# A post-norm layer on one core: the FFN, the projections and V taken out of a stage of their own and put between the two heads' scores of each attention step

## The reference, cut to what matters

```python
# x: 8 batches of 1024 rows, 256 columns; H = 16 heads of D = 16
q, k, v = split(x @ w_qkv.T + b_qkv)
q, k = rope(elu(q) + 1), rope(elu(k) + 1)
attn_out = softmax(q @ k.T / sqrt(D)) @ v
x = layernorm(x + attn_out + depthwise_conv3(v) + b_lepe)
h = concatenate([x, -x])                 # k0, k1, k2 are sign matrices
h = relu(s0 * h @ sign(k0)) * 2          # 512 -> 1024
h = relu(s1 * h @ sign(k1)) * 2          # 1024 -> 1024
x = layernorm(x + s2 * h @ sign(k2))     # 1024 -> 256
```

## Time and profile before

| | before |
|---|---|
| median of 3 runs | 2331.88 us (2328.82 to 2332.24) |
| profiled execution, time | 2330.97 us |
| profiled execution, span | 2329.4 us |
| PE busy | 2144.3 us, 92% |
| DVE busy | 1530.3 us, 66% |
| ACT busy | 1429.2 us, 61% |
| POOL busy | 945.1 us, 41% |
| mean granted TensorE clock | 0.960 |

### The profile page before, as it was taken

The page is one execution under the profiler, slowest core; times in us unless marked ns, Lnnn a source line. Parts: engine busy times, 40 slices in busy tenths (PEclk is TensorE's granted clock), DMA queues, the critical chain, the costliest instruction groups (busy, mean ns, idle before and its releaser), DMA issues.

```text
span 2329.4 us, 41754 instructions
## 1 busy us (share of the span) xinstructions
PE 2144.3 (92%) x16960; PEld 835.0 (36%) x16960; DVE 1530.3 (66%) x1694; ACT 1429.2 (61%) x2605; POOL 945.1 (41%) x657
## 2 busy tenths in 40 slices
PE   4699899999899999999999999999999999998977
PEld 2033223542235422452235422354224532243234
DVE  5968798249962799328982499626984288935332
ACT  2067798339872598428883298725985288924921
POOL 1527534660557315662246604573156522500000
PEclk8599899999999999999999999999999999999989
DMA  5001110010100111001100102001110011000000
GB/s 173 23 7 56 34 40 23 19 42 22 58 15 19 49 40 40 17 10 55 59 22 19 41 22 59 15 19 49 40 40 9 18 56 58 22 1 7 20 1 19
DMA packets 40272, 77.81 MB, mean 33 GB/s; under 512 B 15008, under 2 KB 19472, under 8 KB 36880
## 3 DMA queue, kind: packets, MB, share of 16 engines
q1 hardware_dynamic: 34896, 52.07, 7.9%
q0 software_dynamic: 5184, 23.07, 2.7%
HBM read 47.32 MB, written 25.17 MB: 31 GB/s over the span
## 4 chain that ended last, share of the span: by engine, by line
PE 54%; DVE 17%; ACT 17%; issue 6%; DMA 3%; SPq 2%; POOL 1%; ACTq 0%; DVEq 0%; POOLq 0%
PE unit_banks L677 24%; ACT probs L769 14%; DVE maxima L920 12%; PE o_bank L599 9%; PE unit_banks L533 7%; PE unit_banks L688 5%; PE unit_banks L636 4%; PE unit_banks L648 2%; DMA q_stack<-max_rows 2%; DVE stats L1021 1%; PE unit_banks L543 1%; SPq L446 1%; PE unit_banks L626 1%; ACT o_sb L776 1%; PE unit_banks L656 1%
## 5 line engine op out<-in xcount | busy, mean ns | idle before, releaser
L769 ACT ACTIVATE probs<-unit_banks 128x512 f32<-128x512 f32 x2048 | 1087.6, 604 | 267.7 <-PE unit_banks L543 255.5
L920 DVE TENSOR_REDUCE maxima<-unit_banks 128x1 f32<-128x1024 f32 x1024 | 1188.1, 1210 | 88.8 <-PE unit_banks L533 85.8
L533 PE MATMUL unit_banks<-k_stack,q_stack 48*128 48x512 f16 x2048 | 643.9, 397 | 116.6 <-DVE maxima L920 51.7
L543 PE MATMUL unit_banks<-q_stack,k_stack 50*128 50x512 f16 x2048 | 652.1, 392 | 14.2 <-ACT probs L769 11.0
L599 PE MATMUL o_bank<-probs,v_pair 128*32 128x256 f32 x8192 | 656.8, 399 | 0.4 <-ACT probs L769 0.4
L677 PE MATMUL unit_banks<-h0T,w 128*128 128x512 f16 x2048 | 444.7, 379 | 0.0
L980 DVE SCALAR_TENSOR_TENSOR h1T<-unit_banks,h1T 128x1024 f16<-128x1024 f32 x64 | 78.4, 1224 | 414.8 <-ACT h1T L841 414.8
L533 PEld LDWEIGHTS unit_banks<-k_stack,q_stack 48*128 48x128 f16 x2048 | 118.3, 95 | 546.1 <-DVE maxima L920 312.3
L599 PEld LDWEIGHTS o_bank<-probs,v_pair 128*32 128x32 f32 x8192 | 169.6, 109 | 381.4 <-ACT probs L769 245.6
L841 ACT ACTIVATE h1T<-unit_banks 128x1024 f16<-128x1024 f32 x64 | 65.5, 1023 | 388.3 <-PE unit_banks L677 388.3
L677 PEld LDWEIGHTS unit_banks<-h0T,w 128*128 128x128 f16 x2048 | 200.1, 98 | 241.7 <-issue 3.4
(11 more groups left out here) (132 smaller groups left out, 1534.1 us busy)
## 6 DMA issues: line engine op xcount, KB each, us to landing
xT_sb<-in_xT SPq DMA_DIRECT2D x9, 1024.0 KB, 15.7
base<-in_x POOLq DMA_DIRECT2D x8, 1024.0 KB, 5.7
q_stack<-q_scratch SPq DMA_DIRECT2D x128, 64.0 KB, 2.1
k_stack<-k_scratch SPq DMA_DIRECT2D x128, 64.0 KB, 2.1
out<-hres SPq DMA_DIRECT2D x8, 1024.0 KB, 4.4
q_scratch<-parts POOLq DMA_DIRECT2D x14, 512.0 KB, 3.3
k_scratch<-parts POOLq DMA_DIRECT2D x14, 512.0 KB, 3.9
q_stack<-q_scratch SPq DMA_DIRECT2D x128, 32.0 KB, 1.9
```

The costliest lines, as they stand in the source:

```text
L533: return nc.tensor.matmul(units.half(unit[0], unit[1], half), q_stack[row:row + STACK, r, t * P:(t + 1) * P], k_stack[row:row + STACK, r, ...
L543: nc.tensor.matmul(units.half(kind, unit, 0), k_stack[row:end, r, kt * P:(kt + 1) * P], q_stack[row:end, r, half * 512:(half + 1) * 512], ...
L769: nc.scalar.activation(probs[:, 2 * (kt % 2) + h, half * 512:(half + 1) * 512], units.half(kind, unit, 0), ACT.Exp, scale=exp_regs[2 * j + ...
L920: nc.vector.reduce_max(maxima[:, parity, h * T + t:h * T + t + 1], units.both(kind, unit), AXIS_XY)\
```

## The change

The middle stage is gone. A table `DEALT` gives for each of the 512 steps the pieces of dense work that TensorE runs between the scores of the first head and those of the second. Units are one bank each; units of L1 and L2 come in two pieces, in two steps. Q_AT, K_AT and V_AT are the steps of a batch in which the units of the next batch's q, k and V start; the FFN of batch m is dealt over batch m + 1 and the first 14 steps of batch m + 2. In a step with a piece both halves of the weighted V follow after the second head's scores; in a step without, each half follows a head's scores as before.

Score units are single banks: S has a ring of two banks, T one of two, the rest one of three (in the first batch three, three and one). So a row maximum is over 512 columns, and a small reduction joins the two. LEAD is 4 instead of 6. The maxima of a pair are transposed as float32, and scaled and split by VectorE out of PSUM; GpSimd's `split_max` is gone. Three row buffers take turns (`rows_of(m)`) in place of `base` and `hres`. Lepe is done in two halves. The head bounds (`head_bounds`) sum four terms instead of two. The second layer norm of the seventh batch falls into the end stage.

```diff
-LEAD = 6
+LEAD = 4
+BUFFERS = 3
-LEPE_OPS = 7
+LEPE_OPS = 14
+Q_AT, K_AT, V_AT, SCALE_AT = 7, 29, 43, (12, 35)
+STATS_AT = {**{6 + t // 2: (0, t - t % 2) for t in range(0, T, 2)}, 14: (1, 4), 16: (1, 6), 52 + 4: (1, 0), 52 + 6: (1, 2)}
+MOMENTS_AT = {10: 0, 17: 1}
+NORMALISE_AT = ({13: 0, 14: 2, 15: 4, 16: 6}, {20 + t: t for t in range(T)})
+def dealt():
...
+    for c in range(1, NB):
+        b = (c - 1) * BATCH
+        deal(b + Q_AT, proj_units(c, 0))
+        deal(b + SCALE_AT[0], [("scale", c, 0)])
+        deal(b + K_AT, proj_units(c, 1))
+        deal(b + SCALE_AT[1], [("scale", c, 1)])
+        deal(b + V_AT, v_units(c))
+    for m in range(NB - 1):
+        b = (m + 1) * BATCH
+        deal(b + 17, hT_units(m, 0), 2)
+        deal(b + 18, hT_units(m, 1), 2)
+        deal(b + 19, hidden_units("L0", m, 0), 2)
+        if m < TAIL - 1:
+            deal(b + 23, hidden_units("L1", m, 0, range(3)))
+            deal(b + 33, hidden_units("L1", m, 0, range(3, KF)))
+            deal(b + 47, hidden_units("L0", m, 1), 2)
+            deal(b + 51, out_units(m, 0))
+            deal(b + 55, hidden_units("L1", m, 1))
+            deal(b + 75, out_units(m, 1))
+        else:
+            deal(b + 23, hidden_units("L1", m, 0))
+            deal(b + 39, hidden_units("L0", m, 1), 2)
+            deal(b + 43, out_units(m, 0))
+            deal(b + 47, hidden_units("L1", m, 1))
...
+        if s == BATCH:
+            rings = {"S": (0, 1), "T": (2, 3), "": (4, 5, 6)}
...
+            for s in range(STEPS):
+                n, kt = divmod(s, T)
...
+                scores_both(s, 0)
+                for unit in own_units(s):
...
+                for unit, part in DEALT[s]:
+                    dense(unit, part)
+                if s > 0 and not DEALT[s]:
+                    weighted_v(s - 1, 0)
+                    if kt == 0:
+                        weighted_v(s - 1, 1)
+                scores_both(s, 1)
+                if s > 0 and DEALT[s]:
+                    weighted_v(s - 1, 0)
+                    weighted_v(s - 1, 1)
+                elif s > 0 and kt > 0:
+                    weighted_v(s - 1, 1)
...
-                nc.vector.reduce_max(maxima[:, parity, h * T + t:h * T + t + 1], units.both(kind, unit), AXIS_XY)\
-                  .then_inc(units.free_sem(unit), 1)
+                nc.vector.reduce_max(maxima[:, v // T % 2, h * T + t, half:half + 1], units.out(unit), AXIS_X)\
+                  .then_inc(units.free_sem(unit), 1)
...
+            for n in range(NB * PAIRS):
+                b, j = n // PAIRS, n % PAIRS
+                if n + 1 < NB * PAIRS:
+                    load_max(n + 1)
+                load_freed_stack(n)
+                if j == 3 and b >= 2:
+                    store_out(b - 2)
+                if j == 5 and b < NB - 1:
+                    load_edges(b + 1)
```

More of the change, by code:

```diff
@@ L225, in full_sem, with out @@
+        for u, ring, takes, ends in program_order():
+            if takes:
+                self.before[u] = None
+                before = pending[u]
+                if before is not None:
+                    e, n = READERS[before[0]][1], self.nth_free[before]
+                    if n > waited.get(e, 0):
+                        self.before[u] = (e, n)
+                        waited[e] = n
+    def out(self, unit):
+        return self.psum[:, self.bank[unit], :]
     def full_sem(self, unit):
@@ new lines, in project @@
+            def project(unit):
+                _, c, ct, half = unit
+                pe.wait_ge(xT_loaded, (c + 1) * 16)
+                if c == 0 and ct == 2 and half == 0:
+                    pe.wait_ge(w_kv_loaded, 16)
+                units.wait_free(pe, unit)
+                for kc in range(KC):
+                    done = nc.tensor.matmul(units.out(unit), wT_sb[:, kc, ct * P:(ct + 1) * P],
+                                            xT_sb[:, kc, half * 512:(half + 1) * 512],
+                                            start=kc == 0, stop=kc == KC - 1)
+                done.then_inc(units.full_sem(unit), 1)
@@ L860, in _ @@
             act.wait_ge(bias_loaded, 16)
[L861 to L862 removed]
+            for unit in START_UNITS:
+                if unit[0] == "proj":
+                    elu_inputs(unit)
+            for which, w in enumerate((work[:], work_of(0, 1))):
                 act.wait_ge(scale_made, SCALE_OPS[which])
```

1421 lines of the change are left out of this document (648 added, 773 removed).

## The result

The changed kernel took 2267.64 us (median; 2264.38 to 2271.15), against 2330.43 us (2328.82 to 2332.24) for the kernel before, run beside it: a ratio of 0.9737, 95% interval [0.9718, 0.9757]. The forecast was 2207 us, 5.3% less; it became 2.6% less. The time lies inside the range, but half of the forecast gain is missing.

A forecast was written before the change was run, and what follows sets the result against it. Attention nearly fills TensorE and VectorE; with the dense block hidden beside it, TensorE's own work binds. Start 91, batches 225, 239, 1279, 248 and end 123 make 2205 us of span, so 2207 us; range 2150 to 2310.

The forecast's parts named there:

- The dense step: Step carrying a piece: TensorE's scores 1.06, piece 1.73, way back 0.09 and weighted V 1.00 sum to 3.88 us.
- the rival with free switches: Changes of matmul kind cost nothing in dense steps, 0.17 us less each, about 73 us: 2134 us; chance 12%.
- The reductions' spacing of 0.60: VectorE's row maxima over 512 columns start 0.60 us apart, four taking 2.40 us a step against 2.26 before.
- 45 steps of 2.5, 11 of 3.88, head bounds 4, wait 20: 225: First batch after its first pair (45 us): short steps, dense steps, head bounds and a k chain wait, 225 us in all.
- The 20 us that I did add: First batch: GpSimd's k chain ends about 20 us late because steps 33 to 42 are short ones.
- The reading of the earlier trace as a late k chain: TensorE's 21.4 us wait for k_stack in the kernel before, cited beside the first batch's late GpSimd k chain.
- = 253, with the 2.5 of VectorE 256 each: Each of five middle batches: 253 us of summed steps plus 2.5 of VectorE delays, 256 against 272.75; 1279 together.
- Second batch and last: Second batch 239 us, last 243, with 5 us of small VectorE stalls for both, making the last term 248.
- The end, 123 forecast: After the last exponential: 120.2 us before, plus 3 for eight more normalisations; the extra L2 lies in a wait.
- The rival of late chains: GpSimd's k part or layer-norm scales come some 10 us late in every batch, 70 us: 2277 us; chance 15%.
- The rival of the rings: Two-bank score rings set the dense step's pace because VectorE frees banks late, 0.45 us a step: 2400 us; chance 11%.
- the forecast's walk: Dense step traced through the two-bank score rings: S11's bank is free at 4.10 us, just when TensorE wants it.

The follow-up runs named there:

- e9: Changed kernel with each row maximum read over only 256 of the 512 columns: 2205.91 us, ratio 0.9476 to the kernel before.
- e1: Changed kernel with the later batches' rings (two banks S, two T, three for the rest) from the first step: 2243.58 us, ratio 0.9646.
- e2: Changed kernel with the q head bounds moved from step 12 of a batch to step 15: 2249.02 us, ratio 0.9661.
- e3: Changed kernel with the four hT units one in each of steps 15 to 18, not two in 17 and 18: 2253.9 us, ratio 0.9696.
- c3: Changed kernel with the edits of e1 and e3 together, and the q head bounds in step 16: 2218.97 us, ratio 0.9526.
- e5: Changed kernel with each L1 piece doing four of its eight matmuls, half of L1's sum left out: 2088.85 us, ratio 0.8961.
- e4: Changed kernel with the first half of the weighted V ahead of the piece, except in a pair's first step: 2486.5 us, ratio 1.0693.
- e6: Changed kernel with three banks for S and two for the pieces from the second batch on: 2502.59 us, ratio 1.0743.

## Why the prediction was wrong

The direction and the mechanism of the gain (the middle stage's matmuls hidden beside the attention, a dense step bound by TensorE) were right; two terms of the sum were not, the first batch and the five middle ones. Measured is 2.6% less in place of 5.3%.

- **The dense step, right**: 3.88 forecast, 3.93 measured, and bound by TensorE (e9). The switches cost what the earlier trace rows showed; the rival with free switches is out. The reductions' spacing of 0.60 was right as well. An estimate from "VectorE: DVE Perf Modes" of the Trainium skill, "The TRN2 errata", had 0.66 for it; as a spacing that is too high by these rows.
- **"45 steps of 2.5, 11 of 3.88, head bounds 4, wait 20: 225", wrong: the step whose reasoning failed.** I worked out the rings of the scores and counted the pieces' bank nowhere. With one bank a piece waits for ScalarE's or VectorE's read of the one before; the twelve steps with pieces (eleven in the term, one in the first pair) took 86 us in place of 47. Of the 39, 23 are waits for a reader in the waits of this batch, and most of the rest is matmuls at the lower level of the clock, 1.2 GHz, behind such waits. The 20 us that I did add, for the k chain of GpSimd, never came, so the two errors hid each other in part. The rest of the first pair came out 6 us short of the forecast, the other 45 steps 10 over: 23 over net. e1 gives 21 us back.
- **The reading of the earlier trace rows as a late k chain, wrong.** The 21.4 us wait stands at 57 us, in the start stage, and comes back there in the changed kernel (20.7). A row with "6 times, longest 21.4" doesn't say where; a look at its place in the timeline would have. A shorter one did stand in the first batch before, in the timeline of TensorE; the other four, in later batches, took 0.2 to 1.5 us:

```profile
277.18 0.61 PE L533 MATMUL unit_banks<-k_stack,q_stack 48*128 48x512 f16 x1 [11.34 <-DMA k_stack<-k_scratch]
```

So the kernel before did have a late k chain in its first batch; the changed kernel has none there, nor has e1 with its shorter first batch.
- **"= 253, with the 2.5 of VectorE 256 each", mis-sized by 7 us each, 38 in all and so the largest net error**: TensorE's own work is 257.5, not 253 (0.05 more in each dense step, 3, and steps 21 and 50, where two L0 units meet the max rows or the O rows, at 4.9), and its waits 5.5, not 2.5. The waits stand where units of several kinds meet in the ring: the head bounds with L2 (1.4 to 2.8 us a batch, e2), the hT units two and two (1.7 us, e3; 3.1 forecast for such a step, 4.7 measured). I walked the dense step and took the others as sums of durations.
- **Second batch and last, mis-sized**: regular steps without a piece take 2.88 in the mean, 2.62 forecast, which is 3 us for 13 of them; the dense steps' 0.05 makes 2.5; the two meetings 2.7 (251.5 to 248.8 in c3). Some 4 us are left over: about 1.5 stand in steps 11 and 13, 3.6 us each, and the others are not placed, like the 4 of the last batch.
- **The end, 123 forecast, 112.5 measured**: the eight added normalisations lie off the path, the end stage has lost its two waits for a low part, and the seventh batch's L2 fills the wait.
- **The rival of late chains** is out: TensorE has no wait for a DMA in any batch. **The rival of the rings** failed for the dense step as it stands (e9: VectorE with a third less work takes 0.02 us off it; e5: 0.6 us of slack), but the forecast's walk, "it just fits, with no slack", was right around the weighted V: e4 shifts half of it and pays 0.57 us a step.

With the single bank and the two meetings taken out (c3) the span is 2217.7 us, 13 above the forecast 2205. Those 13 are not settled one by one: 10 are over in the second batch, 18.5 in the middle ones (15 of them the 0.05 of each dense step, if it is in all), 3 in the last, and 4 under in the first, 14 at start and end.

## What to carry to other kernels

When work is moved into another stage's steps, count the turns of every ring of buffers that it passes through, step by step where kinds of unit meet, and not for the regular step alone: here the regular step came out within 0.05 us, and the single bank and the meetings, taken out in c3, cost 50 of the 62 us between the forecast span and the measured one. A ring's turn is the latency to the reader, the reader's queue and its duration; a small unit that only takes a turn can put two large ones on the same bank. A wait read from a sum needs its place before it is carried over to another stage.

## What was not expected of the hardware

- Waits of 2.3 us of TensorE, repeated with pieces of 2 us between, can cost more than themselves: at the q pieces the same four matmuls took 3.75 us after the second (1.95 after the first), and the granted clock of that stretch was 0.79. At the k pieces, from 208.03 us on, they still took 1.95 and 1.96 after waits of 1.78, 2.33 and 2.33, and 3.36 only after a third wait of 2.33. In e6 eight matmuls took 2.98 after a single wait of 1.76 us (1.90 without), with a granted clock of 0.62 from 1228.5 to 1231.5; but of the 48 waits of more than 1.5 us that stand ahead of FFN matmuls in e6's trace, only 7 are followed by a piece at the slower pace. What decides it these runs do not show.
- Moving one bank out of seven from the pieces to the scores cost 10% (e6), and three banks for the pieces in place of one, at the price of one bank less for each kind of score, gave 21 us in the first batch alone (e1).
